# An in-place residual add split between DMA and GpSimd, and the end of a period reordered, in a gated group-norm kernel

## The reference

```python
def _gn(v, G=32, eps=1e-5):          # group norm without scale and bias
    g = v.reshape(B_, G, C_ // G, H_, W_)
    m = mean(g, (2, 3, 4)); s = var(g, (2, 3, 4))
    return ((g - m) / sqrt(s + eps)).reshape(v.shape)

def conv_ref(x, W1, W3):
    x = relu(x)
    x = where(max_pixels(x) - mean_pixels(x) < 0.5, 0.0, x)
    bb = 1 - exp(-abs(max_channels(x) - mean_channels(x)))
    x = bb * x
    x_max = max_pixels(x); pooled = mean_pixels(x)
    control1 = sigmoid(pooled @ W1.T)
    control3 = relu(pooled @ W3.T)
    control3 = where(control3 < 1.0, 1.2, control3)
    return where(x < control1 * control3 * x_max, 0.0, x)

out = x + conv_ref(_gn(x), W1, W3)
```

## Time and profile before

| | us |
|---|---|
| median of 3 runs | 1692.47 (1690.44 to 1693.3) |
| the profiled execution, its own time | 1694.59 |
| span of its profile | 1692.8 |
| VectorE busy | 1459.9 (86%) |
| ScalarE busy | 1355.9 (80%) |
| TensorE matmul busy | 1266.6 (75%) |
| GpSimd busy | 610.5 (36%) |

### The profile page before, as it was taken

The page is one execution under the profiler, slowest core; times in us unless marked ns, Lnnn a source line. Parts: engine busy times, 40 slices in busy tenths (PEclk is TensorE's granted clock), DMA queues, the critical chain, the costliest instruction groups (busy, mean ns, idle before and its releaser), DMA issues.

```text
span 1692.8 us, 26138 instructions
## 1 busy us (share of the span) xinstructions
PE 1266.6 (75%) x9888; PEld 883.0 (52%) x9888; DVE 1459.9 (86%) x2192; ACT 1355.9 (80%) x2177; POOL 610.5 (36%) x446
## 2 busy tenths in 40 slices
PE   3788777887777888777788877778877778877761
PEld 1555455555555555455555555555545555555550
DVE  2588889988889898888998888998888989888896
ACT  6788888788888788888878888888888888888821
POOL 0032334442344442244443243443233444224440
PEclk8988888998788998888898888899888899888885
DMA  9259999999999999999999999999999999999973
GB/s 394 112 127 318 340 355 311 291 314 303 338 350 324 287 316 301 339 343 341 299 303 307 316 343 346 299 309 313 311 342 351 318 299 316 292 340 342 302 228 152
DMA packets 93345, 517.64 MB, mean 306 GB/s; under 512 B 10272, under 2 KB 10272, under 8 KB 93216
## 3 DMA queue, kind: packets, MB, share of 16 engines
q1 hardware_dynamic: 75360, 416.38, 61.1%
q0 software_dynamic: 17856, 99.56, 30.1%
HBM read 310.38 MB, written 205.52 MB: 305 GB/s over the span
## 4 chain that ended last, share of the span: by engine, by line
PE 40%; POOL 28%; ACT 20%; DVE 7%; issue 3%; DMA 1%; DVEq 0%; SPq 0%; ACTq 0%
POOL xs L788 25%; PE ps_gate L331 11%; PE ps_gate L298 10%; PE ps_turn L288 8%; ACT rs L482 6%; ACT rs L457 6%; ACT xs L482 4%; PE ps_gate L318 3%; PE ps_gate L360 2%; PE ps_gate L368 2%; POOL rstd L767 2%; PE ps_gate L306 2%; DVE xs L649 2%; ACT junk L433 1%; DVE max_and_mean L632 1%
## 5 line engine op out<-in xcount | busy, mean ns | idle before, releaser
L632 DVE TENSOR_REDUCE max_and_mean<-ps_turn 128x2 f32<-128x1024 f32 x384 | 463.6, 1218 | 31.8 <-PE ps_turn L288 28.1
L288 PE MATMUL ps_turn<-ident,xs 128*128 128x128 f32 (+1 forms) x1600 | 359.6, 311 | 175.2 <-DVE max_and_mean L632 112.0
L788 POOL TENSOR_TENSOR xs<-xs,rs 128x1568 f32<-128x1568 f32 x124 | 433.3, 3531 | 1.8 <-DVE rs L680 1.8
L779 POOL DMA_DIRECT2D xs<-in_x x124 | 111.5, 968 | 889.4 <-DVE xs L680 796.9
L433 ACT ACTIVATE junk<-xs 128x1568 bf16<-128x1568 f32 x256 | 385.4, 1505 | 9.8 <-ACT junk L433 0.4
L318 PE MATMUL ps_gate<-ident,bb 128*128 128x128 f32 (+1 forms) x1600 | 272.2, 332 | 156.3 <-ACT bb L475 150.8
L288 PE MATMUL ps_turn<-ident,rs 128*128 128x128 f32 (+1 forms) x1600 | 345.7, 302 | 0.0
L318 PEld LDWEIGHTS ps_gate<-ident,bb 128*128 128x128 f32 (+1 forms) x1600 | 248.8, 239 | 175.9 <-DVE ymax_parts L649 163.7
L288 PEld LDWEIGHTS ps_turn<-ident,xs 128*128 128x128 f32 (+1 forms) x1600 | 209.0, 155 | 248.2 <-DVE max_and_mean L632 158.4
L649 DVE CUSTOM_DVE_ANT_0 xs<-xs,ps_gate 128x768 f32<-128x768 f32 (+1 forms) x256 | 243.1, 958 | 48.7 <-PE ps_gate L318 48.5
L457 ACT ACTIVATE xs<-xs,shift,rstd 128x3136 f32<-128x3136 f32 x64 | 192.0, 3001 | 86.0 <-POOL shift L771 80.8
(11 more groups left out here) (80 smaller groups left out, 955.7 us busy)
## 6 DMA issues: line engine op xcount, KB each, us to landing
xs<-in_x SPq DMA_DIRECT2D x260, 784.0 KB, 13.7
out<-xs SPq DMA_DIRECT2D x256, 784.0 KB, 8.2
xs<-in_x POOLq DMA_DIRECT2D x124, 784.0 KB, 10.9
rs<-in_L_conv_W SPq DMA_DIRECT2D x2, 1024.0 KB, 17.5
```

The costliest lines, as they stand in the source:

```text
L288: mm = pe.transpose(ps_turn[0:w, n % 2, b - 2 * i, P * t:P * (t + 1)], r_tile(s, t)[:, P * b:P * b + w], ident[:, :])
L632: ins = dve.tensor_reduce(max_and_mean[:, 2 * i:2 * i + 2, 0], ps_turn[:, n % 2, :, :], AX.X, ALU.max)
L779: pool.dma_start(half(x_tile(s - 1, t), h), dram_half(x_tiles, s - 1, t, h), accum_op=ALU.add).then_inc(x_added[(s - 1) % XR][t][h], 16)
L788: pool.tensor_tensor(o, o, half(r_tile(s - 1, t), h), ALU.add).then_inc(added, 1)
```

## The change

Three things.

1. Half (1, 0), the first half of in-place tile 1, no longer gets x by an accumulating DMA. SP loads that half of x by a plain DMA into a scratch tensor, and GpSimd adds it as a fifth add. The scratch is a float32 tensor of 1568 columns that also holds, in other uses, the junk of the squares (now FP8, in the first 784 columns) and the 512 columns of rows. So SP waits until the mean rows and row means of the period are through, and ScalarE waits for the fifth add before it writes there again. The store of (1, 0) and the load that follows it move to the end of SP's order, and the tiles are loaded in the order 2, 0, 3, 1.
2. ScalarE squares the first tile in halves and the three others whole, and the third tile's square moves ahead of the copy of the mean rows. The sign of the row mean is folded into its scale, which removes one GpSimd instruction from the affine steps.
3. At the end of the period ScalarE does three long pool sums and the last gate values ahead of the fourth relu, and VectorE does all four gates of the third pixel group ahead of peaks, margins and fails, and reads the count and settles the channels after the first gate of the last group.

```diff
+AGAIN = 1
-LOAD_ORDER = (2, 0, 1, 3)
+LOAD_ORDER = (2, 0, 3, 1)
...
-        junk = sb("junk", [P, HALF], BF16)
-        rows = sb("rows", [P, C])
+        scratch = sb("scratch", [P, HALF])
+        junk = scratch[:, 0:HW // 4].bitcast(FP8)
+        rows = scratch[:, HALF - C:HALF]
...
             def store(s, t, h):
...
+                elif t == AGAIN and h == 0:
+                    sp.wait_ge(again_added, s + 1)
...
+                sp.wait_ge(means_ready, s + 2)
+                if s + 2 < B:
+                    sp.wait_ge(row_mean_ready, s + 3)
+                sp.dma_start(scratch[:, :], dram_half(x_tiles, s, AGAIN, 0)).then_inc(x_again, 16)
                 store(s, 2, 0)
                 store(s, 0, 0)
                 store(s, 0, 1)
                 store(s, 2, 1)
-                store(s, 1, 0)
                 store(s, 1, 1)
                 reload(2, 0)
                 store(s, 3, 0)
...
                 store(s, 3, 1)
-                reload(1, 0)
                 reload(1, 1)
+                store(s, 1, 0)
                 reload(3, 0)
                 reload(3, 1)
+                reload(1, 0)
...
+            def square(s, t, cols, part):
+                junk_step.wait()
+                junk_step.step(act.activation(junk[:, cols], x_tile(s, t)[:, cols], ACT.Square,
+                                              scale=float(HW) ** -0.5, accum_out=squares[:, part:part + 1],
+                                              saturate=False))
+            def square_tile(s, n):
                 t = LOAD_ORDER[n]
+                wait_loaded(act, s, t)
+                square(s, t, slice(0, HW), t)
...
             for s in range(B):
                 has_next = s + 1 < B
+                if s > 1:
+                    act.wait_ge(again_added, s - 1)
...
                     square_tile(s + 1, 1)
+                    square_tile(s + 1, 2)
                 copy_mean_rows(s)
                 if has_next:
-                    square_tile(s + 1, 2)
+                    square_tile(s + 1, 3)
                 copy_means(s)
                 if has_next:
-                    square_tile(s + 1, 3)
                     row_means(s + 1)
...
                 gate_values(s, 2)
-                pool_sum(s, 0, 0)
+                for t in range(3):
+                    pool_sum(s, 0, t)
+                gate_values(s, 3)
                 if has_next:
                     relu(s + 1, RELU_ORDER[3])
-                gate_values(s, 3)
-                for t in range(1, T):
-                    pool_sum(s, 0, t)
+                pool_sum(s, 0, 3)
...
-                gate(s, 2, 0)
-                gate(s, 2, 1)
-                gate(s, 2, 2)
+                for t in range(T):
+                    gate(s, 2, t)
                 if nxt < B:
                     peaks(nxt)
-                gate(s, 2, 3)
-                if nxt < B:
                     margins(nxt)
                     find_fails(nxt)
                 gate(s, 3, 0)
                 if nxt < B:
                     read_count(nxt)
-                gate(s, 3, 1)
-                if nxt < B:
                     settle_channels(nxt)
-                gate(s, 3, 2)
-                gate(s, 3, 3)
+                for t in range(1, T):
+                    gate(s, 3, t)
...
-                steps.step(pool.tensor_tensor(mrs[:, :], gst[:, 0, :], rstd[:, :], ALU.mult))
-                steps.wait()
-                pool.tensor_scalar(shift[:, :], mrs[:, :], -1.0, 1.0, ALU.mult, ALU.mult).then_inc(affine_ready, 1)
+                pool.tensor_tensor(shift[:, :], gst[:, 0, :], rstd[:, :], ALU.mult).then_inc(affine_ready, 1)
...
-                        for h in range(2):
+                        for h in range(1 if t == AGAIN else 0, 2):
                             pool.dma_start(half(x_tile(s - 1, t), h), dram_half(x_tiles, s - 1, t, h),
                                            accum_op=ALU.add).then_inc(x_added[(s - 1) % XR][t][h], 16)
...
+                    o = half(x_tile(s - 1, AGAIN), 0)
+                    pool.wait_ge(x_again, 16 * s)
+                    pool.tensor_tensor(o, o, scratch[:, :], ALU.add).then_inc(again_added, 1)
```

More of the change, by code:

```diff
@@ L6 @@
 F32 = mybir.dt.float32
-BF16 = mybir.dt.bfloat16
+FP8 = mybir.dt.float8e4
 I32 = mybir.dt.int32
@@ L98, in gated_sparsifier @@
         half_neg = sb("half_neg", [P, T])
-        squares = sb("squares", [P, 2, T])
+        squares = sb("squares", [P, T + 1])
         row_sum = sb("row_sum", [P, 1])
@@ L106, in gated_sparsifier @@
         rstd = sb("rstd", [P, T])
-        mrs = sb("mrs", [P, T])
         shift = sb("shift", [P, T])
@@ L151, in gated_sparsifier @@
                    for p in range(XR)]
+        x_again = sem("x_again")
+        again_added = sem("again_added")
         w_loaded = [sem("w1_loaded"), sem("w3_loaded")]
@@ L342, in group_stats @@
                 pe.matmul(ps_group[:, 0, :], group_pick[:, :], row_mean[:, :], start=True, stop=True)
-                pe.wait_ge(squared, 2 * T * (s + 1))
-                for h in range(2):
-                    mm = pe.matmul(ps_group[:, 1, :], group_avg[:, :], squares[:, h, :], start=(h == 0),
-                                   stop=(h == 1), skip_group_check=True)
-                mm.then_inc(group_sums, 1)
+                pe.wait_ge(squared, (T + 1) * (s + 1))
+                first = LOAD_ORDER[0]
+                pe.matmul(ps_group[:, 1, :], group_avg[:, :], squares[:, 0:T], start=True, stop=False,
+                          skip_group_check=True)
+                pe.matmul(ps_group[:, 1, first:first + 1], group_avg[:, :], squares[:, T:T + 1],
+                          start=False, stop=True, skip_group_check=True).then_inc(group_sums, 1)
             def count_fails(s):
@@ L427, in _, with square_half @@
             junk_step = Steps(act, squared)
-            def square_half(s, n, h):
-                t = LOAD_ORDER[n]
[L431 to L438, removed]
+            def square(s, t, cols, part):
[3 more added lines that the diff above has]
+                                              saturate=False))
+            def square_half(s, h):
+                t = LOAD_ORDER[0]
+                act.wait_ge(x_loaded[s % XR][t][h], 16 * (s // XR + 1))
+                square(s, t, slice(HALF * h, HALF * (h + 1)), t if h == 0 else T)
+            def square_tile(s, n):
+                t = LOAD_ORDER[n]
+                wait_loaded(act, s, t)
+                square(s, t, slice(0, HW), t)
             def row_means(s):
@@ L443, in row_means @@
                 steps.step(act.activation(junk[:, 0:XCHUNK], ps_rowsum, ACT.Identity,
-                                          scale=1.0 / (PER_GROUP * HW), accum_out=row_sum[:, :]))
+                                          scale=-1.0 / (PER_GROUP * HW), accum_out=row_sum[:, :],
+                                          saturate=False))
                 steps.wait()
@@ L492, in _ @@
             act.wait_ge(consts_ready, 1)
-            for n in range(T):
+            for h in range(2):
+                square_half(0, h)
+            for n in range(1, T):
                 square_tile(0, n)
@@ L502, in _ @@
                 has_next = s + 1 < B
+                if s > 1:
+                    act.wait_ge(again_added, s - 1)
                 if has_next:
-                    square_half(s + 1, 0, 0)
+                    square_half(s + 1, 0)
                 if s > 0:
@@ L507, in _ @@
                 if has_next:
-                    square_half(s + 1, 0, 1)
+                    square_half(s + 1, 1)
                 if s > 0:
@@ L537, in _ @@
                         pool_sum(s, j, t)
+            act.wait_ge(again_added, B - 1)
             copy_control(B - 1)
```

## The result

The changed kernel took **1718.7 us** (median of 4 runs, 1718.26 to 1720.52) against 1692.39 for the kernel before beside it: ratio 1.0159, 95% interval 1.0141 to 1.0177. It is 26 us slower, where 1657 (1637 to 1680) was forecast. The profiled execution took 1718.26 (span 1716.4). TensorE's mean granted clock is 0.817 of full speed; it was 0.868.

A forecast was written before the change was run, and what follows sets the result against it. It took the chain of waits as the bound, GpSimd's adds delaying relu(3) and the last spread, DMA close behind. Terms summed to 49.1 us a period against 50.40; 30 x 1.2 = 36 us gained gave 1657 us (1637 to 1680).

The forecast's parts named there:

- The rest of the period: Step following the earlier gate(3, 0) through turns and products to the next logits; new chain 49.1 us against 50.40.
- The turns start 1.3 earlier: TensorE's turns at the period's end were to start 1.3 us earlier, following gate(3, 0) at 1044.0 instead of 1045.32.
- logits to the end of differ(3): First term of the new chain, from the logits' copy to VectorE's last differ: 33.23 us.
- gate values, relu(3): Second term, ScalarE's last gate values and then the fourth relu behind differ(3): 3.8 us.
- peaks to gate(3, 0): Third term, VectorE's first peak to gate(3, 0), without the gate formerly between: 0.95 us.
- gate(3, 0), settling, start of turns: Fourth term, from gate(3, 0) to the first turn, taken from the old order: 2.13 us.
- turns: Fifth term, TensorE's three turns at the period's end, taken from the old order: 5.40 us.
- products: Sixth term, TensorE's control products after the turns, taken from the old order: 1.87 us.
- end of products to the logits: Last term, from the control products' end to the next copy of the logits: 1.76 us.
- The clock: Rival: shorter TensorE idle before the last spread (over 3 us stays) might keep full clock; 1609, or 1641 us; chance 0.11.
- Tile 3 lands late: Rival at tile 3's square: landings later than the 0.3 us cover lose time each period; up to 1707 us; chance 0.20.
- The reorder gives back what it takes: Rival: later relu(3) delays the peaks more than worked out, period stays the chain through VectorE; 1692 us; chance 0.07.

The follow-up runs named there:

- e11: Kernel after with 18 more unread TensorE matmuls a period at the period's end and eight more ahead of the third turn: 1671.0 us.
- e7: Kernel before with only settle_channels moved ahead of gate(3, 1), right behind the count: 1720.7 us.
- e5: Kernel after with settle_channels back behind gate(3, 1) and 18 more unread TensorE matmuls a period: 1673.6 us.
- e12: Kernel after with settle_channels behind gate(3, 1), squares of tiles 3 and 1 behind the mean rows' and means' copies, 18 unread matmuls a period: 1634.5 us.
- e1: Kernel after with settle_channels back behind gate(3, 1): 1668.9 us.
- e9: Kernel before with ScalarE's and VectorE's new end of the period, but settle_channels behind gate(3, 1): 1652.4 us.
- e3: Kernel before with only ScalarE's and VectorE's new end of the period; no whole squares, plain load or fifth add: 1714.9 us.
- e8: Kernel after with settle_channels behind gate(3, 1) and squares of tiles 3 and 1 behind the mean rows' and means' copies: 1648.2 us.
- e2: Kernel after with ScalarE's and VectorE's old end of the period; whole squares, plain load, fifth add and new load order stay: 1714.4 us.
- e10: Kernel of e2 with the one-word flag allocated ahead of xs: 1709.6 us.

## Why the prediction was wrong

**The step that failed** is in "The rest of the period": the terms 5.40 for the turns and 1.87 for the products (with 0.30 of the 2.13 ahead of them), copied from the old order. "The turns start 1.3 earlier" is right for the first turn of the median period (1.23 earlier) and wrong for the third: in the two periods read it starts 44.83 after the logits before and 44.80 after. I priced the peaks and the spread that the new order moves, and put settle_channels' move from behind gate(3, 1) to directly behind the flag at nothing. It had cost 0.18 because gate(3, 1) covered it. The cover is 1.0 us thick, and without it the work is 1.42 long.

In the period read above the terms are, forecast and then measured:

| term | forecast | measured |
|---|---|---|
| logits to the end of differ(3) | 33.23 | 33.23 |
| gate values, relu(3) | 3.8 | 3.80 |
| peaks to gate(3, 0) | 0.95 | 0.94 |
| gate(3, 0), settling, start of turns | 2.13 | 2.43 |
| turns | 5.40 | 6.34 |
| products | 1.87 | 2.85 |
| end of products to the logits | 1.76 | 1.74 |
| sum | 49.1 | 51.33 |

The first three terms are right to 0.01: the flag is copied 1.23 us earlier in the median period (38.93 against 40.16). Behind it 2.18 us is lost (12.26 against 10.08). The first turn starts as long after the flag as before (1.18 in the median period of both; 1.49 and 1.19 in the two read, which is the 0.30 of the fourth term), but the third turn waits for the later block_max(0).

The loss has two parts, and periods with like clocks separate them. With the third turn and the products at full clock, the way from flag to logits is 10.29 where the call stands directly behind the flag (e11's median, and the fast periods of e7) and 9.51 where it stands behind gate(3, 1) (the medians of e5 and e12): **0.78 is VectorE's idle stretch**. From 10.29 to after's 12.26 is **1.97 for the clock**, which in after is at the 1.2 GHz level from the first turn on through most of the products. e1's median is 9.76, not 9.51, because part of its periods still have a slow third turn; before's 10.08 is such a mixture too, from 9.69 up. In us of the run: moving the call back (e1) wins 49.8; filling TensorE's waits (e11) wins 47.7.

Why the clock is low in all of after's periods is not fully shown. The place of the call matters for it: products of over 2.4 us stand in 4 of 30 periods of before and in 14 of e7, with the old end, and in none of e9's and 29 of e3's, with the new one. But the wait ahead of the third turn does not decide it alone, as the 16 fast periods of e7 show, and what the new end adds to it is open.

The Trainium skill, *Advanced Engine Details and Errata* (Sequencer Loop), says that the sequencer pushes an engine instruction into a queue and runs a control instruction itself, and that other engine instructions can be read and queued while it does. The trace agrees for a gate that stands ahead: the same read, compare and branch leave 0.18 us idle with a gate ahead of them (before) and 1.41 without (e7). The gate behind the branch did not start during them in either.

**The other steps.** Right: relu(3) waits no longer for the add; in the period read, the last spread starts 34.20 after the logits (1003.73 - 969.53, forecast 34.2); peaks wait 0.35 (forecast about 0.5); the fifth add (3.53) is hidden and the gates beside it take 0.94; the accumulating queue's share fell by a quarter, and an accumulating half still costs 0.226 x 1716.4 / 93 = 4.17 us of DMA time. The scratch lands 8.7 us after its issue, hidden. The forecast that the end's new order is worth about 39 us holds where its failed step is undone: e9 is 40.0 faster than before. That the two agree so closely is in part luck: of e9's 1.26 a period in the mean, 1.00 is gained ahead of the flag, where 1.3 was forecast, and 0.26 behind it, where nothing was.

**The rivals.** *The clock* came out with the opposite sign. TensorE's wait ahead of the last spread shrank even more than said, from 4.84 to 2.09 in the periods read ("over 3 us stays" is wrong: the spread before it ends 1.28 later), yet the mean clock fell from 0.868 to 0.817, and a new wait opened ahead of the third turn. *Tile 3 lands late* is true and was masked: in after the squares wait for DMA 4.5 us in all, because everything else is late. In e1 they wait 57.0 us, in e11, whose periods are short too, 52.2. e1 against e8, which moves the squares of tiles 3 and 1, prices it at 20.7 us, 0.7 a period where I had taken off 0.1; the squares that I had let stand ahead of the mean rows' copy carry the delay to VectorE's differ. *The reorder gives back what it takes* had the right sign, but placed the delay in relu(3) and the peaks, where none arose.

**Costed at nothing, and wrong under the old end:** whole squares, plain load and fifth add. With the new end they bring 4.2 us (e8 against e9); with the old end, and with the squares ahead of the mean rows' copy, they lose 22 us (e2). The flag is copied 0.29 sooner than before there, and the way from it to the logits is 1.19 longer (11.27 against 10.08), 0.88 of which is the slower read. Moving the flag to another address (e10) did not cure it. It is not slow because the fifth add runs beside it: in the period read of e2 that add ends at 1003.2, five microseconds before the flag. Why the read is slow in this combination stays open.

## What to carry to other kernels

## What the runs showed of the hardware

The read of one word into a VectorE register took 0.30 to 0.32 us in the median, the register operation behind it 0.18, and the whole settling left the engine idle for 1.42 us with nothing ahead of it. The same read took 1.19 us in e2 and 1.07 in e10; it was not expected and is not explained.

A pause of 0.70 us, between turns that already ran at the 1.2 GHz level, was followed in after by a third turn and most of the sixteen products at that level (2.84 us for the products), in all 30 periods; with no pause the products of the period read in before ran in 1.87. The pause does not decide it: in 16 periods of e7 one of 0.70 to 0.90, behind a second turn at the lower level too, was followed by a third turn (1.02) and products (1.90) at full clock. Eighteen matmuls a period that nobody reads were worth 0.7% in the kernel before, and with eight more 2.8% in after. They gave nothing in e5, where a DMA set the pace.

A ScalarE square of 128x3136 into FP8 took 2.82 us, two halves 1.50 each.
